# The last rows of a fused feed-forward kernel: who adds them and who stores them, and the order of its first stage

## The chip, the cores and the metric

The kernel runs on one core of a Trainium2 chip. The metric is device time in microseconds for one execution, the median of several. For the kernel before it is 422.24 us, the median of three runs (420.89 to 422.67).

## What is computed

There are 128 x 32 = 4096 rows ("tokens") of 256 float32 values. Cut to what matters, the reference is:

```
# first half: x = x + ffn0(cond0(x))
xt     = einsum('bct,bcd->bdt', x, W0[subject]) + bias          # 32 x 32 mix per batch element
scores = softmax(xt @ gate.T); top 2 of 8 experts per row
y      = sum over the two: weight * (silu(xt@w1e.T) * (xt@w3e.T)) @ w2e.T      # inner width 176
z      = (silu(xt@sw1.T) * (xt@sw3.T)) @ sw2.T                                 # shared expert, width 352
x      = x + y + z
# second half: x = x + ffn1(cond1(x))
H      = x @ W.T + scale * (x @ A[adapter].T) @ Bm[adapter].T
act    = gelu(fp8(H) @ fp8(wg0)) * (fp8(H) @ fp8(wg1))          # hidden width 1024
out    = x + fp8(act) @ fp8(wl)
```

The float32 products are done as three products of a high and a low part; those of the last block are in fp8.

## The kernel before, in words

A tile is 128 rows; four tiles (`GT`) are a group, and there are eight groups (`GROUPS`). Each engine has its own instruction stream, written out by hand in the order in which it is to run, and the streams meet only at semaphores. TensorE is PE, VectorE is DVE, ScalarE is ACT, GpSimd is POOL, SyncE is SP; SP and ACT can each issue DMAs on a queue of their own. The order within each stream is fixed by the source: no scheduler moves anything.

**The first stage** (0 to about 40 us) mixes the rows with `W0` and makes the router's scores. SP issues the loads: the table, group 0 of `x` as one DMA of 512 KB (line 304), a first part of the constants, groups 1 to 4, shared weights, the other groups. ACT issues four small loads (lines 465 to 468). DVE makes one block of mixing weights per group (`wrow`, `add_rows`, line 723) and counts `rows_ready`. PE begins with products of ones, whose result nobody reads (`ones`, lines 1209 to 1211): 37 of them, then the bias products, then 6, then `condition(0)` (32 small products per group, line 1177), then 14. Then for i = 0 to 6 it runs `condition(i+1)`, the transposes of group i (`transpose_xt`, line 1187) and from i = 1 `router(i-1)` (line 1197). `condition(i)` waits for the weights of its group and for its rows (`x_in[i]`). ACT evicts: `conditioned(i)` writes `xtr` (line 476), `keep_xT(i)` writes the transposed rows `xtT` (line 490); `router(i)` waits for `keep_xT(i)`. After the loop PE starts the shared expert of group 0 (`shared_up(0, parts)`, lines 1165 to 1167) in six parts, and between the first parts stand the transposes of group 7, `router(6)`, `logits(0)` (a transpose of the raw scores of groups 0 to 3, line 1205), `router(7)` and `logits(1)`. DVE reads the logits in `shifted(0)` and `shifted(1)` (lines 817 and 818); `shifted(0)` stands behind `shared_x_lo(1)` (line 735) and `routed_weight_lo(0)` (line 802). After `shifted(1)` a long series of small dependent DVE steps picks the experts.

**The middle** (the shared and the routed experts, about 40 to 270 us) is not touched by the change.

**The last stage** runs the second half group by group. For a group g, PE makes the up products (`ffn_up`, line 1439), ACT and DVE make the activation, PE makes the down product for two halves of the group of two tiles each (`ffn_down`, line 1454, into banks 6 and 7), ACT copies each half to `ob` (`down_out`, line 662), POOL adds `xm` and writes `fin` (`final`, line 437, count `fin_ready`), and SP stores the whole group, 512 KB, when both halves are there (line 361). The second half of group 6's down product is spread over the chunks of group 7. POOL waits with the second half of group 6 until DVE has made its last activation piece (`act8_ready`, line 434). The last group is cut in three pieces (`LAST`: tiles 0 and 1, tile 2, tile 3); PE makes them in `last_down` (line 1484), ACT copies them in `last_out` (line 672), DVE adds them (line 1156, count `last_ready`), and SP stores each (line 364). SP then waits for all stores (lines 365 and 366), and the kernel ends. `fin` has two places, one for even and one for odd groups; the place of a group is free when the store of the group two before has landed (`o_out`).

Of the kernel before, what the change touches and what calls it, by code (L numbers as in the profile page):

```python
# [12 lines left out]
ALU = mybir.AluOpType  # L13
# [7 lines left out]
TILES = TOK // P  # L21
GT = 4
GTOK = GT * P
GROUPS = TILES // GT
# [11 lines left out]
HC = HID // P  # L36
# [9 lines left out]
WARM = 22  # L46
# [22 lines left out]
def adaln_ffn(nc, front_in, pick_in, adapters, consts, table, x, gate, sw13, sw2, rw13, rw2, l1w, scal, wgate, wlin, out, kept, slots_out):  # L69
# [6 lines left out]
    with ctx:  # L76
# [10 lines left out]
        def sem(name):  # L87
            return ctx.enter_context(nc.semaphore(name))
# [175 lines left out]
        def s(name):  # L264
            if name not in S:
                S[name] = sem(name)
            return S[name]

        for name in ("ids_in front_in pick_in table_in const_in shapes_in gate_in sw_in hot_ready rows_ready c_link c_prep out_ready bias_made bias_ready "
                     "cond_done xt_ready T_done xtT_ready gate_spread raw_done raw_kept logit_psum "  # L270
                     "m_sub m_exp r_ob r_rank r_digits r_lanes r_places r_listed r_perm r_expert sw_hi sw_split "
                     "r_equal r_scaled xs_hi xs_split g_done u_done sil_ready h_ready hh_ready hs_split z_done z_added "
                     "rw_hi rw_split "
                     "xr_T xr_hi xr_split up_done silr_ready hr_ready hr_T hr_hi hr_split y_done y_kept "
                     "l1_in l1_hi w_cast l1_ready y_stored "
                     "comb_a comb_done xm_T xm_hi xm_split xa_done xa_m xa_hi xa_split H_done h8_ready "
                     "gate_done up2_done gel_ready ff1_ready act_ready act8_ready down_done act8_used ob_ready fin_ready last_ready").split():
            s(name)
        x_in = [sem(f"x_in{g}") for g in range(GROUPS)]
        rw_in = [sem(f"rw_in{e}") for e in range(E)]  # L280
        kept_early = [sem(f"kept_early{g}") for g in range(GROUPS - 2)]
# [19 lines left out]
        def _(sp):  # L301
            sp.dma_start(tabr[:, :, :].rearrange("p j e -> p (j e)"), table).then_inc(s("table_in"), 16)

            sp.dma_start(xres[:, 0:GT, :], x_t[0]).then_inc(x_in[0], 16)
            sp.dma_start(cst[:, 0:C_BLK], consts[:, 0:C_BLK]).then_inc(s("shapes_in"), 16)
            def load_x(g):
                sp.dma_start(xres[:, g * GT:(g + 1) * GT, :], x_t[g]).then_inc(x_in[g], 16)
# [48 lines left out]
                sp.wait_ge(y_out[k], 16 * PAIRS // 2)  # L356
            sp.sem_inc(s("y_stored"), 1)  # L357

            for g in range(GROUPS - 1):
                sp.wait_ge(s("fin_ready"), g * 2 + 2)  # L360
                sp.dma_start(out_t[g], fin[:, g % 2]).then_inc(o_out[g % 2], 16)
            for n, (j0, j1, _) in enumerate(LAST):
                sp.wait_ge(s("last_ready"), n + 1)
                sp.dma_start(out_t[GROUPS - 1][:, j0:j1, :], fin[:, 1, j0:j1, :]).then_inc(o_out[1], 16)
            sp.wait_ge(o_out[0], 16 * GROUPS // 2)
            sp.wait_ge(o_out[1], 16 * (GROUPS // 2 - 1 + len(LAST)))


# [1 line left out]
        def _(pool):  # L370
# [57 lines left out]

            def final(g):

                for h in range(2):
                    pool.wait_ge(s("ob_ready"), g * 2 + h + 1)
                    if g == GROUPS - 2 and h:
                        pool.wait_ge(s("act8_ready"), GROUPS * HC)
                    if h == 0 and g >= 2:
                        pool.wait_ge(o_out[g % 2], 16 * (g // 2))
                    pool.tensor_tensor(fin[:, g % 2, 2 * h:2 * h + 2, :].rearrange("p a b -> p (a b)"),  # L437
                                       xm[:, g % 2, 2 * h:2 * h + 2, :].rearrange("p a b -> p (a b)"),
                                       ob[:, 2 * h:2 * h + 2, :].rearrange("p a b -> p (a b)"), ALU.add
                                       ).then_inc(s("fin_ready"), 1)  # L440
# [21 lines left out]
        def _(act):  # L462


            act.dma_start(front[:, :], front_in).then_inc(s("front_in"), 16)
            act.dma_start(pick[:, :], pick_in).then_inc(s("pick_in"), 16)
            act.dma_start(gatew[:, :, :], gate).then_inc(s("gate_in"), 16)
            act.dma_start(scl[:, :], scal).then_inc(s("gate_in"), 16)

# [195 lines left out]
            def last_out():  # L665

                g = GROUPS - 1
                down_out(g - 1, 1)
                for n, (j0, j1, b) in enumerate(LAST):
                    act.wait_ge(s("fin_ready"), g * 2 - 1 if n == 0 else g * 2)  # L670
                    act.wait_ge(s("down_done"), g * 2 + n + 1)
                    act.activation(ob[:, j0:j1, :].rearrange("p a b -> p (a b)"),
                                   bank[b][:, 0:(j1 - j0) * D], ACT.Copy).then_inc(s("ob_ready"), 1)

            def ffn(g, first=False, last=False):

# [21 lines left out]
        def _(dve):  # L698
# [116 lines left out]
            def shifted(h):  # L815
# [3 lines left out]
                                         half(s1, h).rearrange("p (m j) -> p m j", m=HALF).unsqueeze(3).broadcast_to([P, HALF, GT, E]),  # L819
                                         ALU.subtract)  # L820

            shared_x_lo(1)
            routed_weight_lo(0)
            shifted(0)
            dve.wait_ge(kept_early[2], 16)
            hidden_mul(0, 0)
            shifted(1).then_inc(s("m_sub"), 1)
# [322 lines left out]
            for g in range(1, GROUPS - 1):  # L1150
                ffn(g, g % 2, False, False)
            ffn(GROUPS - 1, 1, False, True)
            dve.wait_ge(o_out[1], 16 * (GROUPS // 2 - 1))
            for n, (j0, j1, _) in enumerate(LAST):
                dve.wait_ge(s("ob_ready"), 2 * GROUPS - 1 + n)
# [6 lines left out]
        def _(pe):  # L1162
# [5 lines left out]

            def condition(i):
                pe.wait_ge(s("rows_ready"), i + 1)  # L1170
                pe.wait_ge(x_in[i], 16)
                for b in range(BPT):
                    if i >= 1:
                        pe.wait_ge(s("xt_ready"), (i - 1) * BPT + b + 1)
                    rows = slice(b * CH, (b + 1) * CH)
                    for j in range(GT):
                        ins = pe.matmul(bank[b][j * CH:(j + 1) * CH, 0:D], wrow[rows, i * GT + j, :], xres[rows, i * GT + j, :],
                                        start=True, stop=True, tile_position=(b * CH, j * CH))
                    ins.then_inc(s("cond_done"), 1)
# [30 lines left out]
                for _ in range(n):  # L1210
                    pe.matmul(bank[7][:, 0:P], onesb[:, :], onesb[:, :], start=True, stop=True)

            ones(WARM + WARM // 2 + 4)
            pe.wait_ge(s("out_ready"), 1)
            for j in range(GT):
                ins = pe.matmul(bank[5][j * CH:(j + 1) * CH, 0:TILES], pick[:, BATCH:BATCH + CH].bitcast(F32),
                                hot_out[:, j * TILES:(j + 1) * TILES], start=True, stop=True, tile_position=(0, j * CH))
            ins.then_inc(s("bias_made"), 1)
            ones(6)
            condition(0)  # L1220
            ones(WARM // 2 + 3)
            for i in range(GROUPS - 1):
                condition(i + 1)
                if i == 0:
                    pe.wait_ge(s("shapes_in"), 16)
                transpose_xt(i)
                if i == 1:
                    pe.wait_ge(s("gate_spread"), 1 + HALF)
                if i >= 1:
                    router(i - 1)  # L1230

            def ranks():

# [39 lines left out]
            def shared_down(i, buffers=hidden_s, first=False, chunks=range(3)):  # L1273
# [3 lines left out]
                for c in chunks:  # L1277
                    rows = SCH[c][1]
                    pe.wait_ge(s("hs_split"), i * 3 + c + 1)
                    for j in range(GT):  # L1280
# [4 lines left out]
                        if c == 2 and j % 2 == 1:  # L1285
                            ins.then_inc(s("z_done"), 1)

            pe.wait_ge(s("sw_split"), KC)
            pe.wait_ge(s("xt_ready"), TILES - 3)
            shared_up(0, True, parts=[0])  # L1290
            transpose_xt(GROUPS - 1)
            router(GROUPS - 2)
            logits(0)
            shared_up(0, True, parts=[1])
            router(GROUPS - 1)
            shared_up(0, True, parts=[2])
# [305 lines left out]
```

## Time and profile before

| | us |
|---|---|
| median of three runs | 422.24 (420.89 to 422.67) |
| the profiled execution | 422.06 |
| its span, first to last instruction | 420.2 |
| granted TensorE clock, mean | 1.000 of full speed |
| DVE busy | 312.7 (74%) |
| ACT busy | 249.1 (59%) |
| POOL busy | 191.5 (46%) |
| HBM read, written | 32.18 MB, 17.69 MB |

Times in the profile count from the span's start. An engine's busy time is the time in which it had an instruction under way; matmuls are pipelined, so PE's busy time is not PE at its peak. In a timeline row stand the start, the duration, the engine and line, the operation, what it writes and reads, the count of instructions merged in the row and, in brackets, the idle time before it with what ended it. The time and the span differ by what lies around the first and the last instruction.

### The profile page before, as it was taken

Reading aid. Unit: us, or ns where it says so; the run is one execution under the profiler, and the core shown is the slowest. Engines: PE = TensorE matmul, PEld = TensorE weight load, DVE = VectorE, ACT = ScalarE, POOL = GpSimd, SP = SyncE. Lnnn points to the kernel's source line nnn. Section 1 sums busy time; section 2 is a strip of 40 time slices with the busy share of each in tenths; the row PEclk is TensorE's granted clock in tenths of the full one; section 3 lists DMA queues with packets and bytes.
Section 4 is the critical chain, followed back from the end, with each engine's and each line's share of the span. In section 5 each row is a group of like instructions: output and inputs, shape, how many; then the busy total and the mean of one; then the engine's idle time right before and its main releaser. Section 6 shows DMA issues by size and latency. Waiting matters only on the chain.

```text
span 420.2 us, 8696 instructions
## 1 busy us (share of the span) xinstructions
PE 407.9 (97%) x2956; PEld 332.7 (79%) x2956; DVE 312.7 (74%) x732; ACT 249.1 (59%) x552; POOL 191.5 (46%) x195
## 2 busy tenths in 40 slices
PE   7899999999999999999999999999999999999994
PEld 6467788888899999999999998875575755757663
DVE  6987999997976766666666655769778787787853
ACT  3996566475356666556555644337558475484763
POOL 3320079701764454445445005637567575575011
PEclk9999999999999999999999999999999999999999
DMA  7999300000365555466465422312232243231102
GB/s 229 376 369 367 96 0 2 1 2 11 96 197 158 168 167 166 147 181 162 145 182 153 124 76 78 87 50 77 88 89 91 60 126 91 87 94 57 51 2 101
DMA packets 37258, 50.44 MB, mean 120 GB/s; under 512 B 4472, under 2 KB 30464, under 8 KB 37216
## 3 DMA queue, kind: packets, MB, share of 16 engines
q1 hardware_dynamic: 30288, 32.15, 22.7%
q0 software_dynamic: 6480, 17.70, 15.7%
q8 instruction: 26, 0.43, 0.4%
q14 instruction: 16, 0.13, 0.1%
q10 hardware_dynamic: 448, 0.03, 0.1%
HBM read 32.18 MB, written 17.69 MB: 119 GB/s over the span
## 4 chain that ended last, share of the span: by engine, by line
PE 83%; DVE 10%; ACT 4%; issue 1%; DMA 1%; DVEq 0%; ACTq 0%
PE bank L1165 17%; PE bank L1167 16%; PE bank L1166 16%; PE bank L1439 13%; PE bank L1454 6%; PE bank L1328 4%; PE bank L1367 2%; PE bank L1366 2%; PE bank L1348 2%; PE bank L1405 2%; ACT xtr L476 1%; DVE hsl L790 1%; DVE hsf L783 1%; PE bank L1187 1%; ACT xtT L490 1%
## 5 line engine op out<-in xcount | busy, mean ns | idle before, releaser
L412 POOL DMA_INDIRECT xg<-kept,perm x71 | 68.6, 966 | 82.9 <-PE bank L1328 50.0
L1439 PE MATMUL bank<-h,wg 128*128 128x512 fp8e4 x256 | 62.0, 381 | 0.2 <-ACT ff L656 0.2
L419 POOL DMA_INDIRECT ga<-slots_out,slot x32 | 32.8, 1025 | 37.3 <-SPq L357 21.2
L1165 PE MATMUL bank<-w13h,xgl 128*128 x142 | 48.9, 344 | 0.1
L991 DVE TENSOR_TENSOR hrl<-bank,hrh 128x256 fp32r<-128x256 f32 (+1 forms) x36 | 15.2, 421 | 44.3 <-ACT hrh L595 44.3
L1439 PEld LDWEIGHTS bank<-h,wg 128*128 128x128 fp8e4 x256 | 22.6, 98 | 31.5 <-ACT ff L656 12.5
L1167 PE MATMUL bank<-w13h,xgh 128*128 x142 | 45.6, 321 | 0.0
L1166 PE MATMUL bank<-w13l,xgh 128*128 x142 | 45.6, 321 | 0.0
L654 ACT ACTIVATE gel<-bank 128x512 bf16<-128x512 f32 x64 | 39.7, 620 | 6.7 <-PE bank L1439 3.5
L419 POOL DMA_INDIRECT gb<-slots_out,slot x32 | 37.6, 1174 | 9.8 <-issue 9.8
L401 POOL TENSOR_SCALAR places<-cst,placef 128x72 f16<-128x72 f32 x28 | 26.1, 950 | 31.8 <-DVE placef L878 31.8
L605 ACT ACTIVATE yr<-bank 128x512 f32<-128x512 f32 (+1 forms) x36 | 21.3, 591 | 32.2 <-PE bank L1367 32.2
L656 ACT ACTIVATE ff<-bank 128x512 bf16<-128x512 f32 x64 | 40.1, 627 | 0.0
L1087 DVE TENSOR_TENSOR actb<-gel,ff 128x512 bf16<-128x512 bf16 x64 | 27.5, 429 | 15.4 <-ACT ff L656 15.3
L1165 PE MATMUL bank<-xsh,sw13l 128*118 128x512 f32 (+1 forms) x96 | 38.6, 402 | 0.0
L437 POOL TENSOR_TENSOR fin<-xm,ob 128x512 f32<-128x512 f32 x14 | 16.1, 1152 | 47.7 <-ACT ob L662 38.8
L1167 PE MATMUL bank<-xsh,sw13h 128*118 128x512 f32 (+1 forms) x96 | 37.8, 394 | 0.0
L590 ACT ACTIVATE silr<-bank 128x176 f32<-128x176 f32 x71 | 23.2, 327 | 20.3 <-PE bank L1167 20.1
L1454 PE MATMUL bank<-wl,act 128*128 128x256 fp8e4 x224 | 28.9, 273 | 0.0
L1166 PE MATMUL bank<-xtL,sw13h 128*118 128x512 f32 (+1 forms) x72 | 28.4, 394 | 0.0
L517 ACT ACTIVATE hsh<-hsf 118x512 fp32r<-118x512 f32 (+1 forms) x18 | 11.4, 632 | 28.2 <-DVE hsf L783 26.5
L1454 PEld LDWEIGHTS bank<-wl,act 128*128 128x128 fp8e4 x224 | 21.3, 98 | 8.5 <-issue 1.8
(198 smaller groups left out, 1164.4 us busy)
## 6 DMA issues: line engine op xcount, KB each, us to landing
slots_out<-yr SPq DMA_DIRECT2D x35, 256.0 KB, 2.1
xres<-in_x SPq DMA_DIRECT2D x8, 512.0 KB, 9.8
kept<-xtr SPq DMA_DIRECT2D x7, 512.0 KB, 8.9
out_x<-fin SPq DMA_DIRECT2D x7, 512.0 KB, 2.8
w13raw<-in_rw SPq DMA_DIRECT2D x8, 352.0 KB, 5.0
w2raw<-in_rw SPq DMA_DIRECT2D x8, 256.0 KB, 6.5
wgst<-in_wgate SPq DMA_DIRECT2D x16, 128.0 KB, 2.6
xg<-kept,perm POOLq DMA_INDIRECT x71
```

What stands on the lines that cost most here:

```text
L401: pool.tensor_scalar(places[:, c, :], cst[:, C_J:C_J + SLOT_TILES], placef[:, c:c + 1], cst[:, C_TOKEN + t:C_TOKEN + t + 1], ALU.is_equal, ...
L412: pool.indirect_dma_start(out=xg[i % GATHERS][:, j, :], out_offset=None, in_=kept, in_offset=bass.IndirectOffsetOnAxis(perm[:, 2 * i + j:2 ...
L419: pool.indirect_dma_start(out=buf[:, g % 2, j, :], out_offset=None, in_=slots_out, in_offset=bass.IndirectOffsetOnAxis(slot[:, k, g * GT + ...
L590: act.activation(silr[:, j, :], bank[j][:, 0:INNER], ACT.Silu).then_inc(s("silr_ready"), 1)
L654: act.activation(gel[:, b, :], bank[b][:, :], ACT.Gelu_apprx_tanh).then_inc(s("gel_ready"), 1)
L656: act.activation(ff1[:, b, :], bank[2 + b][:, :], ACT.Copy).then_inc(s("ff1_ready"), 1)
L1087: dve.tensor_tensor(actb[:, c % 4, :], gel[:, b, :], ff1[:, b, :], ALU.mult).then_inc(s("act_ready"), 1)
L1165: pe.matmul(dst, al, bh, start=first, stop=False, skip_group_check=True)
L1166: pe.matmul(dst, ah, bl, start=False, stop=False, skip_group_check=True)
L1167: return pe.matmul(dst, ah, bh, start=False, stop=last, skip_group_check=True)
L1439: ins = pe.matmul(bank[bk][:, :], wg8[:, kk, half, c * P:(c + 1) * P], h8[:, k, kk, :], start=(kk == 0), stop=(kk == KC - 1))
L1454: ins = pe.matmul(bank[6 + half][:, (j % 2) * D:(j % 2 + 1) * D], act8[:, c, j * P:(j + 1) * P], wl8[:, c, :], start=(c == 0 and j % 2 == ...
```

## The change

Three parts of the code change.

1. Store of group 6. SP stores tiles 0 and 1 (256 KB) as soon as POOL has added them, and tiles 2 and 3 when a new count, `half_ready`, is 1. That second half is now added by DVE, behind its last activation piece of group 7 and ahead of the last group's pieces; POOL no longer does it. ACT, which overwrites `ob`'s second half with the pieces 1 and 2 of the last group, waits for `half_ready` where it waited for `fin_ready`.
2. Piece 1 of the last group (tile 2, 128 KB) is stored by ACT's queue, behind ACT's last copy; SP stores pieces 0 and 2.
3. First stage. Group 0 of `x` is loaded in halves, one by SP and one by ACT's queue ahead of `gate` and `scal`. PE's ones are 33, 4 and 11 in place of 37, 6 and 14. `logits(0)` and `router(6)` stand ahead of `shared_up(0)` and of the transposes of group 7. DVE runs `shifted(0)` ahead of `shared_x_lo(1)` and `routed_weight_lo(0)`.

```diff
@@ sync: loads
-            sp.dma_start(xres[:, 0:GT, :], x_t[0]).then_inc(x_in[0], 16)
+            sp.dma_start(xres[:, 0:2, :], x_t[0][:, 0:2, :]).then_inc(x_first[0], 16)
@@ sync: stores
-            for g in range(GROUPS - 1):
+            for g in range(GROUPS - 2):
                 sp.wait_ge(s("fin_ready"), g * 2 + 2)
                 sp.dma_start(out_t[g], fin[:, g % 2]).then_inc(o_out[g % 2], 16)
+            sp.wait_ge(s("fin_ready"), 2 * GROUPS - 3)
+            sp.dma_start(out_t[GROUPS - 2][:, 0:2, :], fin[:, 0, 0:2, :]).then_inc(o_out[0], 16)
+            sp.wait_ge(s("half_ready"), 1)
+            sp.dma_start(out_t[GROUPS - 2][:, 2:GT, :], fin[:, 0, 2:GT, :]).then_inc(o_out[0], 16)
             for n, (j0, j1, _) in enumerate(LAST):
+                if n == 1:
+                    continue
                 sp.wait_ge(s("last_ready"), n + 1)
                 sp.dma_start(out_t[GROUPS - 1][:, j0:j1, :], fin[:, 1, j0:j1, :]).then_inc(o_out[1], 16)
-            sp.wait_ge(o_out[0], 16 * GROUPS // 2)
+            sp.wait_ge(o_out[0], 16 * (GROUPS // 2 + 1))
@@ gpsimd: final
-                for h in range(2):
+                for h in range(2 if g < GROUPS - 2 else 1):
                     pool.wait_ge(s("ob_ready"), g * 2 + h + 1)
-                    if g == GROUPS - 2 and h:
-                        pool.wait_ge(s("act8_ready"), GROUPS * HC)
@@ scalar
             act.dma_start(pick[:, :], pick_in).then_inc(s("pick_in"), 16)
+            act.dma_start(xres[:, 2:GT, :], x_t[0][:, 2:GT, :]).then_inc(x_first[1], 16)
             act.dma_start(gatew[:, :, :], gate).then_inc(s("gate_in"), 16)
...
-                    act.wait_ge(s("fin_ready"), g * 2 - 1 if n == 0 else g * 2)
+                    if n == 0:
+                        act.wait_ge(s("fin_ready"), g * 2 - 1)
+                    else:
+                        act.wait_ge(s("half_ready"), 1)
                     act.wait_ge(s("down_done"), g * 2 + n + 1)
...
+                j0, j1, _ = LAST[1]
+                act.wait_ge(s("last_ready"), 2)
+                act.dma_start(out_t[g][:, j0:j1, :], fin[:, 1, j0:j1, :]).then_inc(o_out[1], 16)
@@ vector
+            shifted(0)
             shared_x_lo(1)
             routed_weight_lo(0)
-            shifted(0)
...
             ffn(GROUPS - 1, 1, False, True)
+            dve.wait_ge(s("ob_ready"), 2 * GROUPS - 2)
+            dve.wait_ge(o_out[0], 16 * (GROUPS // 2 - 1))
+            dve.tensor_tensor(fin[:, 0, 2:GT, :]..., xm[:, 0, 2:GT, :]..., ob[:, 2:GT, :]..., ALU.add).then_inc(s("half_ready"), 1)
@@ tensor
-                pe.wait_ge(x_in[i], 16)
+                for sem_in in x_first if i == 0 else [x_in[i]]:
+                    pe.wait_ge(sem_in, 16)
...
-            ones(WARM + WARM // 2 + 4)
+            ones(WARM + WARM // 2)
...
-            ones(6)
+            ones(4)
             condition(0)
-            ones(WARM // 2 + 3)
+            ones(WARM // 2)
...
                     router(i - 1)
+                if i == GROUPS - 2:
+                    logits(0)
...
+            router(GROUPS - 2)
             pe.wait_ge(s("sw_split"), KC)
-            pe.wait_ge(s("xt_ready"), TILES - 3)
             shared_up(0, True, parts=[0])
             transpose_xt(GROUPS - 1)
-            router(GROUPS - 2)
-            logits(0)
             shared_up(0, True, parts=[1])
```

## Rows read from the trace of the kernel before

**Rows 1.** The page, busy time by engine: us (share of the span) xinstructions.
```profile
PE 407.9 (97%) x2956; PEld 332.7 (79%) x2956; DVE 312.7 (74%) x732; ACT 249.1 (59%) x552; POOL 191.5 (46%) x195
```

**Rows 2.** The chain that ended last, its end: start us, us, what.
```profile
413.81 0.60 ACT ob L672
...
414.51 1.40 DVE fin L1156 x3
```

**Rows 3.** The timeline of the last 18 us: start us, us, engine, line, operation.
```profile
403.26 1.15 POOL L437 TENSOR_TENSOR fin<-xm,ob 128x512 f32<-128x512 f32 x1 [14.48 <-ACT ob L662]
...
411.87 0.63 ACT L662 ACTIVATE ob<-bank 128x512 bf16<-128x512 f32 x1
...
412.39 0.75 DVE L1100 TENSOR_SCALAR act<-actb 128x512 fp8e4<-128x512 bf16 x2
413.29 1.15 POOL L437 TENSOR_TENSOR fin<-xm,ob 128x512 f32<-128x512 f32 x1 [8.87 <-DVE act L1100]
413.81 1.04 ACT L672 ACTIVATE ob<-bank 128x512 bf16<-128x512 f32 x2 [1.31 <-PE bank L1484]
414.46 0.37 SPq L361 DMA_DIRECT2D out_x<-fin  x1
...
415.07 0.38 ACT L672 ACTIVATE ob<-bank 128x256 bf16<-128x256 f32 x1 [0.22 <-issue]
415.23 1.60 SPq L364 DMA_DIRECT2D out_x<-fin  x3
```

**Rows 4.** Waits of SP's queue, last 21 us: total, times, longest.
```profile
SPq L366 <- DMA out_x<-fin: 2.3, 1, 2.3
```

**Rows 5.** DMA issues of the last 21 us: count, KB each, median us to landing.
```profile
out_x<-fin SPq DMA_DIRECT2D x1, 512.0 KB, 3.4
out_x<-fin SPq DMA_DIRECT2D x1, 256.0 KB, 2.9
out_x<-fin SPq DMA_DIRECT2D x2, 128.0 KB, 2.9
```

**Rows 6.** Stretches of the end; the last two columns are DMA share and GB/s.
```profile
417.50:418.00 0.50, 0.00 (x0) 0.00 (x0) 0.00 (x0) 0.00 (x0) 0.00 (x0) 1.00 1.10 385
418.00:418.50 0.50, 0.00 (x0) 0.00 (x0) 0.00 (x0) 0.00 (x0) 0.00 (x0) 1.00 0.36 123
```

**Rows 7.** The page, DMA issues: a store of 256 KB in the middle.
```profile
slots_out<-yr SPq DMA_DIRECT2D x35, 256.0 KB, 2.1
```

**Rows 8.** The timeline of the first 24 us.
```profile
0.98 4.13 PE L1211 MATMUL bank<-onesb 128*128 128x128 bf16 x37 [0.98 <-POOL onesb L371]
...
1.77 0.36 ACTq L467 DMA_DIRECT2D gatew<-in_gate  x1
...
6.30 0.98 PE L1177 MATMUL bank<-xres,wrow 32*32 32x256 f32 x32
...
7.22 0.96 PE L1211 MATMUL bank<-onesb 128*128 128x128 bf16 x14
...
9.19 0.73 PE L1177 MATMUL bank<-xres,wrow 32*32 32x256 f32 x32 [1.01 <-DVE wrow L723]
...
14.07 0.21 PEld L1177 LDWEIGHTS bank<-xres,wrow 32*32 32x32 f32 x27 [0.20 <-DVE wrow L723]
```

**Rows 9.** The chain that ended last, two pieces of the first stage.
```profile
8.84 0.34 issue
...
27.55 0.60 issue
```

**Rows 10.** DMA issues between 1 and 2 us: the load of group 0.
```profile
xres<-in_x SPq DMA_DIRECT2D x1, 512.0 KB, 3.5
```

**Rows 11.** DMA issues between 2.0 and 2.4 us: the load of group 1.
```profile
xres<-in_x SPq DMA_DIRECT2D x1, 512.0 KB, 6.9
```

**Rows 12.** The timelines of ACT and of DVE, 20 to 36 us.
```profile
27.09 1.18 ACT L490 ACTIVATE xtT<-bank 128x512 f32<-128x512 f32 x2
...
35.52 0.29 DVE L817 TENSOR_REDUCE s<-bank 128x16 f32<-128x128 f32 x1 [1.48 <-PE bank L1205]
```

More of the change, by code:

```diff
@@ L276, in adaln_ffn @@
                      "comb_a comb_done xm_T xm_hi xm_split xa_done xa_m xa_hi xa_split H_done h8_ready "
-                     "gate_done up2_done gel_ready ff1_ready act_ready act8_ready down_done act8_used ob_ready fin_ready last_ready").split():
+                     "gate_done up2_done gel_ready ff1_ready act_ready act8_ready down_done act8_used ob_ready fin_ready half_ready last_ready").split():
             s(name)
+        x_first = [sem(f"x_first{h}") for h in range(2)]
         x_in = [sem(f"x_in{g}") for g in range(GROUPS)]
@@ L1152, in _ @@
             ffn(GROUPS - 1, 1, False, True)
+            dve.wait_ge(s("ob_ready"), 2 * GROUPS - 2)
+            dve.wait_ge(o_out[0], 16 * (GROUPS // 2 - 1))
+            dve.tensor_tensor(fin[:, 0, 2:GT, :].rearrange("p a b -> p (a b)"), xm[:, 0, 2:GT, :].rearrange("p a b -> p (a b)"),
+                              ob[:, 2:GT, :].rearrange("p a b -> p (a b)"), ALU.add).then_inc(s("half_ready"), 1)
             dve.wait_ge(o_out[1], 16 * (GROUPS // 2 - 1))
```

## The prediction, made before the changed kernel ran

> **What bounds the kernel now.** I read the page first: PE has work 97% of the span [rows 1], no other engine comes near, so what is not on PE's path costs only where PE's chain begins or ends. Then the chain of waits, from its end: ScalarE's copy of the last group, three adds by VectorE, and after them nothing of an engine [rows 2]. The last add ends at 414.51 + 1.40 = 415.91, the span at 420.2: 4.3 us in which only stores run. The waits of SP's queue say the same: its last wait lasts 2.3 us [rows 4] and begins when its last issue is over, 415.23 + 1.60 = 416.83 [rows 3], so the last store lands at 419.1. The landings and the stretches say why it takes so long: at 414.46 the whole of group 6 is issued (512 KB, lands after 3.4 us), then pieces of 256, 128 and 128 KB, which take 2.9 us each [rows 3, 5], against 2.1 us for a lone store of 256 KB [rows 7]. The queue is full: 385 GB/s up to 418.0 and then an end at about 418.0 + 0.5 x 0.36 / 1.10 = 418.16 [rows 6]. 1.05 MB at 0.383 MB/us is 2.74 us, so data flows from 415.42 on, 0.96 us behind the first issue. The end of the kernel is a store of 1 MB at full rate, behind PE's last product.
>
> Of the first stage I read the chain and the timeline. Its links alternate between DVE, PE and ACT; two of them are "issue": 0.34 us ahead of condition(1) and 0.60 us within the last router product of the loop [rows 9].
>
> **The change part by part.**
>
> *Group 6 in halves.* POOL's first half is ready at 403.26 + 1.15 = 404.41 [rows 3]; its 256 KB leave while PE multiplies, with no other DMA about, and land within some 2.1 us [rows 7]. At the end 256 KB less are to be moved: 0.262 MB / 0.383 = 0.68 us.
>
> *The second half on VectorE.* DVE's last activation piece ends at 412.39 + 0.75 = 413.14; the copy it needs is there at 411.87 + 0.63 = 412.50 [rows 3]. The add is of the same shape as the first of the three of line 1156, which together take 1.40 for 4 tiles, 2 + 1 + 1 [rows 2]: 0.70. It ends at 413.85, and SP issues at about 413.9 in place of 414.46 (POOL: 413.29 + 1.15 = 414.44). Queued behind it on DVE are the last group's adds, whose first starts at 414.51: 0.66 us of slack, cost 0. PE waits for nothing of it. ACT's copy of piece 0 does not wait for it, piece 1 does, and that one starts near 414.45: slack 0.6. POOL has nothing left. If DVE's casts came late by more than 0.6 us, this add would delay the last group one to one.
>
> *Piece 1 on ACT's queue.* ACT is free at 415.07 + 0.38 = 415.45, the second add is done at 414.51 + 1.05 = 415.56, so ACT issues at 415.6. On SP piece 2 no longer stands behind piece 1: add done at 415.91, issue at 415.95. Before, the three issues filled 1.60 us [rows 3] and the last began near 416.2, some 0.26 us after its data were there.
>
> *The sum at the end.* Half of group 6: data 414.86 to 415.54, out of the way. Piece 0, issued at 415.23: data from 416.19. The three pieces, 0.524 MB, take 1.37 us: end at 417.56 in place of 418.16. (Piece 2 alone would be through at 415.95 + 0.96 + 0.34 = 417.25, so data, not the issue, sets the end.) From the end of data to the landing it was 419.13 - 418.16 = 0.97 before; a lone 256 KB needs 2.1 - 0.96 - 0.68 = 0.46. Landing between 418.02 and 418.53, against 419.13: a gain of 0.6 to 1.1; I take the middle, 0.85. Outer ends: at most 1.4, if the last 128 KB land like a lone store (0.96 + 0.34 + 0.46 behind 415.95 is 417.71); at least 0.3, if they take 2.9 us as before (418.85); and nothing, if a piece takes the 3.4 us of the largest (from 415.6: 419.0). A loss I exclude: every piece is issued no later than before.
>
> The same queue has a row that bears on the part with ACT: the pieces share one full rate [rows 5, 6]. The Trainium skill says so too (DMA: Bandwidth & Descriptors, Issuing engines are not separate DMA queues): issuing from several engines saves only the issuing time. By that rule the move to ACT alone is worth at most the 0.26 us, and, data setting the end, 0 in my sum. [...]
>
> *First stage, loads.* Group 0 needed 3.5 us from its issue at about 1.2 [rows 10], condition(0) starts at 6.30 [rows 8]. Its second half is now issued by ACT at 1.77, where `gate` was, and shares the engines with the same bytes as before: at 5.3 if it takes as long, a slack of 1. `gate` and `scal` move back by one issue (0.36 [rows 8]) and 256 KB; the first use is router(0), after 13. ACT's own work starts one issue later, and it idles then. Group 1 was issued at 2.18 and took 6.9 us [rows 11]: it lands at 9.1, and this, not DVE, is the 0.34 us of "issue" before condition(1) at 9.19 [rows 8, 9]. The bytes ahead of it are the same, so I put the change at 0; ends -0.3 (it comes with the weights at 8.84) and +0.3. Either is taken up later: condition(3) at 14.07 started behind DVE's weights [rows 8]. Cost 0.
>
> *First stage, ones.* 4 + 2 + 3 = 9 products fewer. The first 37 took 4.13 us, 0.11 each, the 14 later ones 0.96, 0.07 each [rows 8]. They are fillers: PE then idles longer, or condition(0) starts up to 0.2 earlier, which nobody needs, since condition(1) waits for its rows. Cost 0, unless the clock answers (below).
>
> *First stage, order.* The same 16 + 1 PE instructions stand earlier; PE's sum is unchanged. router(6) needs ACT's `xtT` of group 6, there at 27.09 + 1.18 = 28.27 [rows 12]. PE left the loop's last router product only at about 28.5, because of the 0.60 us stall [rows 9], and logits(0) stands ahead: no wait. If the stall is gone, PE gains up to 0.6 and waits 0.3 of it again. On DVE shifted(0) comes before work that idled for ACT anyhow; the point that counts is shifted(1), which DVE began at 35.52 after idling 1.48 for PE [rows 12]. It hangs on PE's sum alone. Taken 0, ends -0.6 and +0.3. What would be late next if PE came sooner is that same small-step chain on DVE, so a gain here would reach the end.
>
> **Sum.** 422.06 (the profiled execution, its span 420.2 and 1.9 around it) - 0.85 + 0 = 421.2. The median shown is 0.18 above that execution; I carry this over: **421.4**.
>
> **The rivals.**
>
> *The clock starts late (slower than before).* Place: the first 14 us. Price: the 32 products of condition(0) took 0.98 us, those of condition(1) 0.73; a product of ones took 0.11 and later 0.07, and without the lead-in nearly half [rows 8]. So PE was at the lower of its two levels (1.2 GHz) in the first ones and at 2.4 by 7.2, after 5 us of nearly unbroken products. The changed kernel has 9 fewer, and a gap of 0.6 us or more before the bias products. If the rise came only near 14, PE's part of the 4.9 us between conditions 1 and 3, about half, would take up to twice as long: +2, a little of it absorbed; I take +1.8. Time 421.4 + 1.8 = 423.2. It decides from a loss of 0.85 on. For it: what was taken away is just that lead-in. Against it: 33 ones at the slow rate are still 3.7 us. The Trainium skill (TensorE: Matmul & The Clock Gate, Part 1) states the rule: throttled is the default and activity releases it. The trace agrees with slow products first and fast ones after.
>
> *The stores gain nearly nothing.* The last piece's 2.9 us are latency, not queue: gain 0.3, or 0. For it: a piece of 128 KB and one of 256 took the same 2.9. Against it: the full rate to 418.0. Time 421.8 to 422.2.
>
> *More than the sum.* The end gains 1.4 and the stall at 27.55 goes: 0.6. Time 420.2 to 420.6.
>
> *It does not do what it says.* DVE's extra add lies on the path, since its casts slip: half of group 6 is stored at 414.5 as before. Then only the early 256 KB help; 0.6, time 421.6, within the forecast's range.
>
> **How the numbers follow.** Forecast 0.56 (its own range 420.8 to 421.9), late clock 0.13, no gain 0.17, more 0.14. The range reaches from the full gain to most of the late clock: 420.1 to 422.9. A measurement of this kernel tells about 0.5%, 2.1 us, from no change: faster means below 420.1, slower above 424.4. The forecast and the second rival lie within; a third of the largest gain and some of the noise lie below: 0.10; the worst of the late clock above: 0.06; so 0.84 within.
>
> **What would show it.** Right: an issue of 256 KB near 404.4, one near 413.9, pieces at 415.2, 415.6 (ACT) and 415.95; the full rate ending near 417.6; SP's last wait shorter than 2.3 and ending near 418.3 (plus whatever the first stage shifts); DVE's first add of the last group with idle time before it. condition(1) near 9.2 and shifted(1) near 35.5. Wrong: condition(1)'s 32 products at 0.98 or more, which is the late clock; shifted(1) off by over 0.5; a landing still 2.9 us behind the last issue.

## The result and the profile after

The changed kernel takes 420.23 us (median of 17 runs, 419.04 to 420.92) against 421.69 us for the kernel before in the same rounds (17 runs, 420.79 to 426.59). The ratio of the two is 0.9942, with a 95% interval of 0.9923 to 0.9961: between 1.6 and 3.2 us less. The medians alone are 1.5 us apart; 4 of the 17 runs of the kernel before took more than 423 us, none of the changed kernel more than 421. The forecast was 421.4, a gain of 0.85 us. The time lies in the range, but the gain is nearly three times the forecast one by the ratio and 1.7 times by the medians.

The profiled execution took 419.49 us with a span of 417.6, 2.6 us less than that of the kernel before. The timeline of its end answers to [rows 3]:

```profile
402.44 1.15 POOL L442 TENSOR_TENSOR fin<-xm,ob 128x512 f32<-128x512 f32 x1 [14.48 <-ACT ob L668]
...
403.62 0.37 SPq L364 DMA_DIRECT2D out_x<-fin  x1
...
411.57 0.76 DVE L1112 TENSOR_SCALAR act<-actb 128x512 fp8e4<-128x512 bf16 x2
412.24 0.68 DVE L1167 TENSOR_TENSOR fin<-xm,ob 128x512 f32<-128x512 f32 x1
412.95 0.37 SPq L366 DMA_DIRECT2D out_x<-fin  x1
...
413.69 1.36 DVE L1172 TENSOR_TENSOR fin<-xm,ob 128x512 f32<-128x512 f32 x3 [0.77 <-ACT ob L681]
414.41 1.01 SPq L371 DMA_DIRECT2D out_x<-fin  x2
414.75 0.35 ACTq L685 DMA_DIRECT2D out_x<-fin  x1
```

The instructions are there as foretold: the early half, VectorE's add directly behind its last activation piece, 0.77 us of idle time before the last group's adds (0.66 were expected), the three pieces at their places. The landings of the last stretch, which answer to [rows 5]:

```profile
out_x<-fin SPq DMA_DIRECT2D x2, 256.0 KB, 2.4
out_x<-fin ACTq DMA_DIRECT2D x1, 128.0 KB, 2.1
out_x<-fin SPq DMA_DIRECT2D x1, 128.0 KB, 2.1
```

2.1 us for the last pieces in place of 2.9. And the waits of SP's queue, which answer to [rows 4]:

```profile
SPq L373 <- DMA out_x<-fin: 1.7, 1, 1.7
...
SPq L76 <- PEq L76: 0.2, 1, 0.2
```

The second row has a counterpart in the kernel before that I had not put among the rows: the same view says there

```profile
SPq L76 <- PEq L76: 0.8, 1, 0.8
```

So the kernel before waits 0.8 us at its closing meeting of all engines, after the last store has landed, and the changed one 0.2. Line 76 is where the block closes. The view of that line shows, for the kernel before, what each engine's queue does there (operation, count, duration in ns as min/median/max, start):

```profile
L76 POOLq EVENT_SEMAPHORE  x2: 17/17/17, 420.0 to 420.1; - x2
L76 PEldq DRAIN  x1: 1492/1492/1492, 413.3 to 413.3; - x1
L76 POOLq DRAIN  x1: 6740/6740/6740, 413.3 to 413.3; - x1
...
L76 SPq DRAIN  x1: 7/7/7, 419.4 to 419.4; - x1
```

and for the changed kernel

```profile
L76 POOLq EVENT_SEMAPHORE  x2: 17/17/17, 417.5 to 417.5; - x2
L76 POOLq DRAIN  x1: 6752/6752/6752, 402.4 to 402.4; - x1
...
L76 SPq DRAIN  x1: 7/7/7, 417.4 to 417.4; - x1
```

The reader is to see this: GpSimd's queue closes with a drain (the instruction DRAIN of line 76) of 6.74 us, which the trace has starting beside GpSimd's last add. In the kernel before, that add is the second half of group 6, at 413.29 [rows 3], so the drain ends at 413.3 + 6.7 = 420.0, and GpSimd's next event, which releases all the others, stands at 420.0. SP had been ready since 419.4. The wait's name (PEq) is the one that came last by that view's inference, and misleads: PE's own drain was over at 414.7. In the changed kernel GpSimd's last add is at 402.44, its drain is over at 409.2, and the releasing event follows SP's arrival at once (417.4, 417.5). The end of the kernel before was not held by its stores. All 14 profiles of this case show the same: GpSimd's first event of line 76 stands within 0.05 us behind the later of two points, the end of its own drain and SP's drain.

The first stage, as the chain shows it around the load (it answers to [rows 9]):

```profile
1.77 4.65 DMA xres<-in_x
6.42 0.14 issue
6.56 1.17 PE bank L1194 x32
7.73 1.29 PE bank L1228 x11
9.01 1.44 PE bank L1194 x30
```

The second half of group 0 landed only at 6.42 (4.65 us behind ScalarE's issue), condition(0) waited for it, and the 11 ones, condition(1) and the first transposes ran slowly: 1.29 us for 11 ones is 0.12 each, against 0.07 [rows 8]. The column of the granted clock reads 1.00 for these stretches in both profiles, so that this is the clock is read off the durations. The repeat of the changed kernel (below) shows it directly: there the granted clock was 0.50 from 7.1 to 13.8, the lower of its two levels, and condition(1) and condition(2) took 1.17 and 1.16 us. Before it fell, PE had waited 0.91 us for GpSimd (`hot_out`) and 0.45 us for the second half of group 0. One stretch of that repeat (PE, PEld, DVE, ACT, POOL busy, then the granted clock, DMA share and GB/s):

```profile
10.40:13.80 3.40, 3.40 (x44) 2.26 (x43) 3.33 (x3) 3.06 (x9) 0.10 (x1) 0.50 1.05 398
```

Yet in the changed kernel's profile shifted(1), the point that counts, is earlier. The rows of PE, ScalarE and VectorE, to be held against [rows 8] and [rows 12] (27.09 and 35.52):

```profile
8.94 1.51 PE L1194 MATMUL bank<-xres,wrow 32*32 32x256 f32 x32
...
12.28 0.84 PE L1194 MATMUL bank<-xres,wrow 32*32 32x256 f32 x32
...
26.86 1.22 ACT L496 ACTIVATE xtT<-bank 128x512 f32<-128x512 f32 x2
...
34.92 0.29 DVE L829 TENSOR_REDUCE s<-bank 128x16 f32<-128x128 f32 x1 [1.40 <-PE bank L1222]
```

### The profile page after: what moved, and what is told of

Same layout as the page of the kernel before. It is cut to its first block, busy times and chain, and to the rows that moved or that the text cites. A ratio compares the mean times of both kernels' runs of the same rounds, so it can differ in the third digit from the quotient of the medians.

```text
span 417.6 us, 8680 instructions
## 1 busy us (share of the span) xinstructions
PE 408.6 (98%) x2947; PEld 332.7 (80%) x2947; DVE 313.4 (75%) x733; ACT 248.9 (60%) x552; POOL 190.2 (46%) x194
## 4 chain that ended last, share of the span: by engine, by line
PE 83%; DVE 9%; ACT 5%; DMA 1%; issue 1%; ACTq 0%; DVEq 0%
PE bank L1181 17%; PE bank L1183 16%; PE bank L1182 16%; PE bank L1456 13%; PE bank L1471 6%; PE bank L1345 4%; PE bank L1384 2%; PE bank L1383 2%; PE bank L1365 2%; ACT xtr L482 2%; PE bank L1422 2%; ACT xtT L496 2%; DVE hsl L802 1%; DVE hsf L795 1%; DMA xres<-in_x 1%
## 5 line engine op out<-in xcount | busy, mean ns | idle before, releaser
L442 POOL TENSOR_TENSOR fin<-xm,ob 128x512 f32<-128x512 f32 x13 | 15.0, 1151 | 38.8 <-ACT ob L668 38.8
L523 ACT ACTIVATE hsh<-hsf 118x512 fp32r<-118x512 f32 (+1 forms) x18 | 11.4, 632 | 28.1 <-DVE hsf L795 26.5
```

## The accounts of the two profiled executions

The measure that tells the end apart from everything before it is the time from VectorE's first add of the last group (the start of the row of line 1156 or its successor) to three marks: SP's drain (all stores landed), the end of GpSimd's drain, the end of the span. All from the timelines and the views of line 76; "end" with two decimals is the start of the last closing event, 0.05 us before the end of the span:

```
                                       first add   SP there   span's end   add to SP   add to end
before                                  414.51      419.4      420.2         4.9         5.7
changed                                 413.69      417.4      417.6         3.7         3.9
```

Of the 2.6 us, 1.8 fall behind that add and 0.8 ahead of it (0.6 of these at shifted(1), 0.2 somewhere in the 380 us between). The stores alone moved from 4.87 to 3.73, by 1.1, against a forecast of 0.85 (0.6 to 1.1).

Part of this 1.1 is not the work of the change at the end. The same four stores, with the same code at the end, were over 4.87 us behind the first add in the kernel before, but 4.35 us in the two kernels that have only the changed loads and ones, or the whole changed first stage. Their landings, for the first stage alone, against 3.4, 2.9 and 2.9 in [rows 5]:

```profile
out_x<-fin SPq DMA_DIRECT2D x1, 512.0 KB, 2.9
out_x<-fin SPq DMA_DIRECT2D x1, 256.0 KB, 2.7
out_x<-fin SPq DMA_DIRECT2D x2, 128.0 KB, 2.5
```

The queues show what differs: one packet of 8 KB that carries instructions. In the kernel before it moves at 416.69, in the middle of the stores, and the last packets of the stores trickle out one by one until 418.76, half a microsecond after the full rate has ended [rows 6]; in the kernel with the first stage alone it moves at 414.48, ahead of the stores, and there is no such tail. In the kernel before, the row of the packet between 416.6 and 416.8 (queue, packets, MB, share), and the stretch behind [rows 6]:

```profile
q14 instruction: 1, 0.01, 9.7%
```
```profile
418.50:419.00 0.50, 0.00 (x0) 0.00 (x0) 0.00 (x0) 0.00 (x0) 0.00 (x0) 1.00 0.04 12
```

In the changed kernel it moves at 414.45, ahead of the last group's pieces. So against a kernel with the end as before in which the packet is out of the way too, the change at the end makes the stores 4.35 - 3.73 = 0.6 us shorter, the lower side of the forecast; the other 0.5 us is where that packet happened to fall. No run moved the packet alone, so this stays a reading of the traces.

## The experiments

Two theories after the first four runs. **D**: the end was held by GpSimd's drain, which runs for 5.6 us behind the end of its last instruction; taking its add away is the larger part of the gain, and the stores come second. **S**: the stores held the end, as the prediction has it. For the first stage, **C**: its change gives nothing that can be measured.

### The end alone

```diff
 # the kernel before, with these parts of the change and no other:
+ # SP: group 6 stored in halves; VectorE adds the second half (half_ready); ACT's queue stores piece 1
```

> The kernel before with the stores of the end changed and nothing else: group 6 in halves, its second half added by VectorE, piece 1 stored by ScalarE's queue. Theory A (the end gives more than half of what was measured, because the stores are short of the full rate and the landing is quicker): 1.1 to 1.8 us less than the kernel before (ratio 0.996 to 0.9975), the last landing some 1.15 us sooner after VectorE's first add of the last group than before, and shifted(1) at 35.5 as before. Rival B (most came from the first stage): 0.3 to 0.8 us less.

Measured: 420.12 us, ratio 0.9947 (0.9922 to 0.9972). That is all of the gain, within the interval. From the first add (413.95) to the span's end (418.0) 4.1 us. The upper side of theory A's 1.1 to 1.8 us was passed: 2.2. shifted(1), with the first stage exactly as before, came at 34.95 and not at the expected 35.5: it moves by itself.

### The first stage alone

```diff
+ # x of group 0 in halves, 33/4/11 ones, logits(0) and router(6) ahead of shared_up(0), shifted(0) first
  # end as before
```

> The kernel before with the first stage changed and nothing else. Theory A: 0.5 to 0.7 us less, shifted(1) near 34.9 in place of 35.5, since PE finds no stall and has router(6) and logits(0) behind it; the loss of the late clock (condition(1) and the first transposes at the slow rate) is taken up by ScalarE's cadence. Rival B: 1 us or more less in the median, the long executions of the kernel before (423 to 427 us) being gone. Rival C: no gain, the 0.6 us of the one profile being a stall that comes and goes.

Measured: 421.84 us, ratio 0.9989 (0.9965 to 1.0012). shifted(1) at 35.16. A gain of 0.5 us can't be told from none; the interval reaches to 1.5 us, so it does not exclude rival B (1 us or more) either.

### The order alone

```diff
+ # logits(0) and router(6) ahead of shared_up(0); shifted(0) first on VectorE
  # loads and ones as before
```

> Only the order of PE and VectorE in the first stage: logits(0) and router(6) ahead of shared_up(0), shifted(0) first on VectorE; loads and ones as before. If the order is what gives the first stage's gain: the same 0.6 us less as the whole of the first stage, or 0.1 to 0.3 more, the clock being fast by 7 us. If the gain is only a stall that fell elsewhere: 0, shifted(1) at 35.5 to 35.8.

Measured: 422.43 us, ratio 0.9992 (0.9966 to 1.0018), shifted(1) at 35.19, so neither the gain nor the expected 35.5 to 35.8.

### The loads and the ones alone

```diff
+ # x of group 0 in halves; ones(33), ones(4), ones(11)
  # order as before
```

> Only the loads and the ones of the first stage: group 0 in halves, the second half by ScalarE's queue; 33, 4 and 11 ones; the order as before. Theory A: 0 to 0.3 us more, because condition(1) and the first transposes run at the slow rate and the later stages take most of it up. Rival C (instructions fetched at another time): 0.6 less, the stall at 27.5 gone.

Measured: 421.52 us, ratio 0.9979 (0.9953 to 1.0005), shifted(1) at 35.45 although condition(0) began only at 7.3 and condition(2) at 12.6 (11.4 before). The interval holds 1 as well as a gain of 2 us; nothing in the trace's first stage supports a gain, so I take it as none.

In these three, with the end as before, the span ended 5.67 us behind VectorE's first add (414.12, 415.04 and 414.41 to 419.79, 420.71 and 420.08), to 0.01 us the same as in the kernel before, while SP was ready 4.35, 4.87 and 4.35 behind it. A quantity that stands still while the stores vary by half a microsecond is not set by the stores. That led to theory D.

### GpSimd keeps the add, the stores are changed

```diff
+            sp.wait_ge(s("fin_ready"), 2 * GROUPS - 3)
+            sp.dma_start(out_t[GROUPS - 2][:, 0:2, :], fin[:, 0, 0:2, :]).then_inc(o_out[0], 16)
+            sp.wait_ge(s("fin_ready"), 2 * GROUPS - 2)
+            sp.dma_start(out_t[GROUPS - 2][:, 2:GT, :], fin[:, 0, 2:GT, :]).then_inc(o_out[0], 16)
+            # and piece 1 by ACT's queue; final(6) on GpSimd as before
```

> The kernel before with group 6 stored in halves and piece 1 on ScalarE's queue, but GpSimd still adds the second half, behind VectorE's last activation piece. Theory D (the end is set by GpSimd's closing drain, which ends 6.75 us after the start of its last add, and not by the stores): the stores land some 0.8 us sooner than before, and the time does not move (ratio 0.999 to 1.001); from VectorE's first add of the last group to the end of the span it stays 5.67 us. Rival S (the stores set the end): 0.6 to 1.1 us less, from that add to the end 4.1 to 4.8 us.

Measured: 421.95 us, ratio 0.999 (0.9956 to 1.0024). Its profile, the last add of GpSimd and the first of VectorE, the waits of SP, and line 76:

```profile
413.91 1.15 POOL L443 TENSOR_TENSOR fin<-xm,ob 128x512 f32<-128x512 f32 x1 [8.87 <-DVE act L1109]
...
415.14 1.40 DVE L1165 TENSOR_TENSOR fin<-xm,ob 128x512 f32<-128x512 f32 x3 [1.37 <-ACT ob L678]
```
```profile
SPq L76 <- PEq L76: 1.5, 1, 1.5
```
```profile
L76 POOLq EVENT_SEMAPHORE  x2: 17/17/17, 420.7 to 420.8; - x2
...
L76 POOLq DRAIN  x1: 6743/6743/6743, 413.9 to 413.9; - x1
...
L76 SPq DRAIN  x1: 7/7/7, 419.3 to 419.3; - x1
```

SP is there 4.2 us behind the first add, 0.7 sooner than before; the span ends 5.67 behind it, as before. What the stores gained, SP waits at the close: 1.5 us in place of 0.8. This is theory D's picture: shorter stores, and no earlier end.

### VectorE adds, the stores are as before

```diff
-                for h in range(2):
+                for h in range(2 if g < GROUPS - 2 else 1):          # GpSimd; VectorE adds the other half
+                if g == GROUPS - 2:
+                    sp.wait_ge(s("half_ready"), 1)                    # SP then stores group 6 whole
```

> The kernel before with VectorE adding group 6's second half in GpSimd's place; group 6 is stored whole and all by SP's queue as before, only 0.5 us sooner. Theory D: the drain is over early, the stores become the bound: from VectorE's first add to the end 4.4 to 5.1 us against 5.67, so 0.5 to 1.3 us less than before. Rival S: at most 0.3 us less.

Measured: 421.3 us, ratio 0.9968 (0.9935 to 1.0001). From the first add (414.72) SP is there after 4.15 us and the span ends after 4.3, not 5.67: theory D's mark, a little below its 4.4. The profile decides here, the ratio alone would not: its interval overlaps with that of the run before this one.

This also says how much is whose. In the kernel before, the drain ended the kernel 5.67 us behind the first add, and the stores would have ended it about 0.2 us behind their 4.87. So the drain held the end back by some 0.6 us beyond the stores (an estimate from these numbers). Moving the add gives 1.4 us because it does two things at once: GpSimd's drain leaves the end, and group 6 is stored some 0.6 us sooner, so that the stores are over sooner as well.

### The changed kernel with a tiny late fill by GpSimd

```diff
+            pool.wait_ge(s("act8_ready"), GROUPS * HC)
+            pool.memset(ga[:, 0, 0, 0:8], 0.0)
```

> The changed kernel with one tiny fill (8 floats per partition of a buffer that is dead by then) by GpSimd behind VectorE's last activation piece, where its add stood before; nothing waits for it. Theory D: the drain takes its 6.7 us from there, the span ends about 5.6 us after VectorE's first add of the last group in place of 3.9, and the gain of the change is all but gone: 1.5 to 1.8 us more than the changed kernel, ratio to the kernel before 0.998 to 1.001. Rival S: as the changed kernel, ratio 0.994.

Measured: 422.29 us, ratio 0.9988 (0.9955 to 1.0021), against 0.9942 and, in the repeat below, 0.9947 for the changed kernel. The fill, and line 76:

```profile
413.51 0.11 POOL L465 MEMSET ga<- 128x8 f32 x1 [8.79 <-DVE act L1114]
...
414.82 1.36 DVE L1174 TENSOR_TENSOR fin<-xm,ob 128x512 f32<-128x512 f32 x3 [0.77 <-ACT ob L683]
```
```profile
L76 POOLq EVENT_SEMAPHORE  x2: 17/17/17, 419.2 to 419.3; - x2
L76 POOLq DRAIN  x1: 5668/5668/5668, 413.5 to 413.5; - x1
...
L76 SPq DRAIN  x1: 7/7/7, 418.5 to 418.5; - x1
```

A fill of 0.11 us for which nothing waits holds the end: SP is there at 418.5, the event comes at 419.2. It also sizes the cost: the drain is 5.67 here and 6.74 behind an add of 1.15 us, so it lasts 5.54 and 5.56 us from the end of GpSimd's last instruction (413.62 to 419.16, 414.44 to 420.00). I had taken it as 6.7 whatever stood before it; so from the first add to the end it was 4.5 us, not 5.6, and 0.6 us more than the changed kernel in the profile, not 1.5 to 1.8. The medians differ by more than that, but the time alone shows nothing here: the kernel of the next section, without the fill, took 422.15 us in the same rounds. It is the profile that shows the effect.

### The change of the end without ScalarE's queue

Against the end alone, without ScalarE's three lines:

```diff
-                if n == 1:
-                    continue
```

> The change of the end without ScalarE's queue: group 6 in halves, added by VectorE, all pieces stored by SP. The skill's rule (Trainium skill, DMA: Bandwidth & Descriptors) allows the move to ScalarE's queue the issuing time only: 0 to 0.3 us more than the end change in full; from VectorE's first add to the end 4.0 to 4.4 us against 3.9 to 4.1. If ScalarE's queue mattered more: 0.5 us more or above.

Measured: 422.15 us, ratio 0.9975 (0.9944 to 1.0006). From the first add (416.49) to SP 3.96, to the end 4.1, against 3.92 and 4.1 with ScalarE's queue: at this end the queue is worth nothing that the profile shows. The ratio is less sure; the execution that was profiled reached the last stage 1.5 us later than the others, ahead of anything that was changed.

### The changed kernel again, and three neighbours

The changed kernel, run again:

> The changed kernel once more, beside the other three of this call, on their chip. Ratio to the kernel before 0.992 to 0.996; from VectorE's first add of the last group to the span's end 3.8 to 4.1 us.

Measured: 420.23 us, ratio 0.9947 (0.9928 to 0.9967); from the first add (414.74) to the end 3.9.

The changed kernel with the last three adds taken straight from PSUM:

```diff
-                    act.activation(ob[:, j0:j1, :]..., bank[b][:, 0:(j1 - j0) * D], ACT.Copy).then_inc(s("ob_ready"), 1)
...
-                dve.wait_ge(s("ob_ready"), 2 * GROUPS - 1 + n)
+                dve.wait_ge(s("down_done"), 2 * (GROUPS - 1) + n + 1)
                 dve.tensor_tensor(fin[:, 1, j0:j1, :]..., xm[:, 1, j0:j1, :]...,
-                                  ob[:, j0:j1, :]..., ALU.add).then_inc(s("last_ready"), 1)
+                                  bank[b][:, 0:(j1 - j0) * D], ALU.add).then_inc(s("last_ready"), 1)
```

> The changed kernel with the three last adds taken by VectorE straight from PSUM: ScalarE's three copies fall away (the last group's result is then not rounded to bf16 before the add). If the stores behind the last add now set the end: the adds start where ScalarE's first copy started, the last ends 0.4 to 0.6 us sooner, and 0.4 to 0.6 us less than the changed kernel. If something else holds the end: 0.

Measured: 419.73 us, ratio 0.9939 (0.9914 to 0.9965): 0.5 us less in the median than the changed kernel, as expected, though the intervals overlap. The adds now follow each other on VectorE without a gap:

```profile
413.19 0.68 DVE L1159 TENSOR_TENSOR fin<-xm,ob 128x512 f32<-128x512 f32 x1
413.90 0.37 SPq L366 DMA_DIRECT2D out_x<-fin  x1
413.95 1.35 DVE L1164 TENSOR_TENSOR fin<-xm,bank 128x512 f32<-128x512 f32 x3
```

Last store landed and closed 3.9 us behind the first of these adds, as in the changed kernel; what is won is the step through ScalarE.

The same with the first stage as it was:

> The same direct adds with the change of the end only, the first stage as in the kernel before. Against e10 this is the first stage's change alone with the end no longer held by GpSimd. Theory C (the first stage gives nothing that can be measured): within 0.2% of e10. If the first stage gives the 0.6 us of the one profile: 0.5 to 0.7 us more than e10.

Measured: 419.64 us, ratio 0.9934 (0.9907 to 0.9961), within 0.1 us of the run with the first stage changed. shifted(1) stands at 34.77 here and at 34.98 there. This is what theory C expects: with GpSimd's drain out of the way, no gain of the first stage's change is seen. With 9 runs each and intervals of 0.3% either way, a gain of 0.6 us is not excluded by these times alone.

The kernel before with ScalarE's queue alone:

```diff
+                j0, j1, _ = LAST[1]
+                act.wait_ge(s("last_ready"), 2)
+                act.dma_start(out_t[g][:, j0:j1, :], fin[:, 1, j0:j1, :]).then_inc(o_out[1], 16)   # alone
```

> The kernel before with nothing but piece 1 of the last group stored by ScalarE's queue. Theory D: the span still ends 5.67 us after VectorE's first add of the last group (GpSimd's closing drain), ratio 0.999 to 1.001. Rival S: 0.3 us less.

Measured: 422.29 us, ratio 1.0004 (0.9982 to 1.0025). The span ends 5.67 us behind the first add (414.68 to 420.35). The drain held the end here, so the time could not have shown what the queue is worth; the stores can: SP was there 4.88 us behind the first add, 4.87 in the kernel before.

The best version of these is the changed end with the direct adds (419.64 us with the first stage as it was, 419.73 with it changed, which can't be told apart); it skips one rounding to bf16.

## Why the prediction was wrong, by its own steps

**"In which only stores run."** This is the step that failed. I read 4.3 us between the last add and the span's end as stores, from a wait of 2.3 us that ended at 419.1, and so took the 1.1 us from there to 420.2 for something that would move with the stores. It did not: 5.6 us of drain behind GpSimd's last add, 414.44 to 420.00, lay beside the stores and ended later. The part of the change that I priced at 0 gain ("POOL has nothing left", stores issued 0.5 sooner) is the one that freed the end. In the profiles, GpSimd keeping its add with all the stores changed left the 5.67 us from the first add to the end as they were (ratio 0.999, 0.9956 to 1.0024); GpSimd without it and the stores whole gave 4.3; a dead fill put GpSimd back in the way, 4.5 in place of 3.9.

**The stores.** That fewer bytes at the end land sooner was right. Expected: landing 0.6 to 1.1 us sooner, 0.85 taken; measured from the first add to SP: 4.87 to 3.73, so 1.1, and 0.7 in the run where only the stores changed. The last pieces landed in 2.1 us, as a lone store does. Of the 1.1, about 0.5 is the packet of instructions that fell among the stores of the kernel before, which the forecast did not see: it took the data to end at 418.16 and 0.97 us from there to the landing, but packets of the stores went on until 418.76. And had the drain stayed, none of it would have been seen. Compared to the sum: 0.85 forecast behind the first add, 1.8 measured.

**ScalarE's queue.** 0 forecast with the data setting the end, 0 measured, two ways, each from the first add to SP (alone: 4.88 against 4.87 us; with and without it at the changed end: 3.92 and 3.96). The Trainium skill's rule (DMA: Bandwidth & Descriptors, Issuing engines are not separate DMA queues), that issuing from several engines saves only the issuing time, agrees with these numbers.

**VectorE's add.** 0.70 forecast, 0.68 measured; slack 0.66 forecast, 0.77 measured. Right.

**First stage, loads and ones.** The late clock, which I gave 0.13, did come in the changed kernel: 0.12 us for a product of ones at 7.7, condition(1) at 1.51 us, fast rows only from 12.3. Its price was wrong: not +1.8, but no loss that a run shows. The second half of group 0 took 4.65 us and not the 3.5 I lent it, so condition(0) waited 0.44 us for it. ScalarE's first eviction of transposes came 0.9 us late (12.18 against 11.32), and at group 6 the changed kernel was 0.2 us ahead (26.86 against 27.09). In the kernel before, PE had stood still for 0.65 us within condition(3):

```profile
15.41 0.62 PE L1177 MATMUL bank<-xres,wrow 32*32 32x256 f32 x5 [0.65 <-issue]
```

That stall is large enough for most of the catching up in this pair. It is not the whole story: the end alone, with the early clock and no such stall, was at 27.13 as well, and the loads and ones alone still 0.7 us late (27.84). What takes up the delay was not isolated.

**First stage, order.** Taken 0, and the 0.6 us of the profiled pair is the stall at 27.55 that I named as the gain's upper end. It is no property of the order: in eight profiles with the order as before, shifted(1) stood at 34.47 to 35.52, in six with the new order at 34.92 to 35.25. That the profiled pair differs by 0.6 us there is chance.

**The class.** "Within 0.5%" had 0.84. With 1.8 us in place of 0.85 behind the first add the sum would have been 420.3, and 420.4 with the median's 0.18. The measured 420.23 is just inside the bound of 420.1, but that bound was drawn from 422.24; against the kernel before in the same rounds the ratio is 0.9942, outside 0.5%. The rival "more than the sum", 420.2 to 420.6, has the right number by luck: of its two terms the landing gained 1.1 and not 1.4, and would have shown nothing with the drain in place, and the stall is none of the change's doing, for the end alone gave the whole gain (0.9947) with the first stage as it was.

Left open: why executions of the kernel before now and then take 423 to 428 us. The changed kernel's 29 runs have none above 420.92, but the four kernels from "GpSimd keeps the add" to "without ScalarE's queue" each have some above 425; they ran on another chip beside each other, and each holds part of the changed end, the one with the late fill all of it. So the change of the end is not shown as what removes them. They may also be why the ratio (2.4 us) and the medians (1.5 us) put the gain at different sizes.

## What to carry to other kernels

The end of a kernel is a race between every engine's last instruction plus its closing drain, and not only the last store: look at the view of the line where the block closes, and hold each engine's last instruction plus its drain against the landing of the last store. In this kernel GpSimd's last instruction had to end 5.6 us or more before the stores were over. An add handed to an engine that is idle there gave 1.4 us behind the first add with the stores whole; the reordering of the stores without it gave none. A distance that stays equal to 0.01 us across variants points to a fixed latency, whatever name the wait carries. And when the same stores take half a microsecond more in one profile than in another, look at which packets stood among them before crediting the change.

## What the runs showed of the hardware

GpSimd's closing drain lasts 5.54 to 5.56 us from the end of its last instruction in all 14 profiles, after an add of 1.15 us (6.74 in all) as after a fill of 0.11 us (5.67); in the changed kernel, whose last GpSimd add ended at 403.6, it took as long (6.75), only beside other work. PE's took 1.49 us, ScalarE's 0.15 to 0.40, VectorE's 0.46 to 0.71, SP's 0.01. Whether one small store left by ScalarE's queue or by SP's made no difference (4.88 against 4.87 us from the first add to SP, 3.92 against 3.96); a store of 128 KB landed 2.1 to 2.3 us behind its issue when some 0.5 MB was issued within 0.7 us, and 2.5 to 3.2 when 1 MB was issued within 1.8 us: 2.5 where the 8 KB packet of instructions moved ahead of the stores, 2.9 to 3.2 where it moved among them.
